# Group norms 1 to 3: mean squares kept in the statistics tile and summed by a second product on TensorE, with the engines' orders written anew

## The reference

```
x = x + block0(gn(x))   # gated line recurrences over rows and columns, with a layer norm
x = x + block1(gn(x))   # maxima of shifted images, 1x1 conv, batch norm, gelu
x = x + block2(gn(x))   # depthwise 11x11 conv with a kernel made of 4 bumps
x = x + block3(gn(x))   # 1x1 conv, 8x8 real FFT filter, 3x3 depthwise, gelu gate, 1x1 conv
def gn(v, G=32, eps=1e-05):
    g = v.reshape(B, G, C // G, H, W)
    m = mean(g, axis=(2, 3, 4)); s = var(g, axis=(2, 3, 4))
    return (g - m) / sqrt(s + eps)
```

## Time and profile before

| | |
|---|---|
| median of 3 runs | 204.95 us (204.21, 204.95, 208.93) |
| the profiled execution | 203.61 us |
| its span in the trace | 201.8 us |
| PE / PEld busy | 172.9 us (86%) / 122.1 us (61%) |
| DVE busy | 171.9 us (85%) |
| ACT / POOL busy | 124.1 us (62%) / 85.8 us (42%) |

### The profile page before, as it was taken

How to read it: one execution, slowest core, us unless ns; L and a number is a source line. 1 busy time by engine, 2 the same in 40 slices (tenths; PEclk the granted TensorE clock), 3 DMA queues, 4 the chain that set the end, 5 groups by cost and what they waited for, 6 DMA issues and landing times. The chain is left out here.

```text
span 201.8 us, 3245 instructions
## 1 busy us (share of the span) xinstructions
PE 172.9 (86%) x852; PEld 122.1 (61%) x852; DVE 171.9 (85%) x436; ACT 124.1 (62%) x272; POOL 85.8 (42%) x173
## 2 busy tenths in 40 slices
PE   2998997988998999999999797499998999986192
PEld 1566564743453884797975486198687788844130
DVE  6678996659987979798999999968999989988792
ACT  3255698669988959779589694053755655361510
POOL 7636237222443244337674777543247490220000
PEclk9999999699799999999999999969999999999559
DMA  5991000000001000000000100011000000101002
GB/s 147 287 229 39 13 16 15 20 20 15 7 8 29 1 10 11 10 20 8 9 7 0 39 0 0 2 44 41 0 3 0 22 17 3 39 2 39 0 0 78
DMA packets 8273, 6.29 MB, mean 31 GB/s; under 512 B 6080, under 2 KB 6848, under 8 KB 8160
## 3 DMA queue, kind: packets, MB, share of 16 engines
q1 hardware_dynamic: 8256, 6.09, 12.0%
HBM read 2.94 MB, written 1.57 MB: 22 GB/s over the span
## 5 line engine op out<-in xcount | busy, mean ns | idle before, releaser
L476 PE MATMUL bank<-xw,bumps 128*128 128x192 f32 x256 | 46.5, 337 | 0.3 <-DVE x L1456 0.3
L476 PEld LDWEIGHTS bank<-xw,bumps 128*128 128x128 f32 x256 | 43.3, 196 | 3.5 <-issue 3.5
L1081 POOL TENSOR_TENSOR msq<-moments 96x2 f32<-96x2 f32 x24 | 7.2, 300 | 45.6 <-DVE moments L1267 45.4
L1128 POOL TENSOR_TENSOR xw<-x_pix,weights 128x384 f32<-128x384 f32 x18 | 17.8, 1014 | 5.6 <-ACT x_pix L840 5.6
L1478 DVE SCALAR_TENSOR_TENSOR bank<-above,weights,bank 112x512 f32<-112x512 f32 x24 | 18.0, 750 | 0.7
L1478 DVE SCALAR_TENSOR_TENSOR bank<-below,weights,bank 112x512 f32<-112x512 f32 x24 | 18.0, 752 | 0.5
L1253 DVE BATCH_NORM_STATS2 stats<-x 96x6 f32<-96x256 f32 x48 | 17.7, 411 | 0.2
L1085 POOL TENSOR_TENSOR rstd<-gvar,weights 96x2 f32<-96x2 f32 x24 | 16.6, 694 | 1.9
L1092 POOL TENSOR_TENSOR ln_rstd<-ln_var,weights 128x4 f32<-128x4 f32 x8 | 8.6, 1078 | 16.6 <-ACT squared L779 16.6
L513 PE MATMUL bank<-prod,weights 128*128 128x512 f32 x16 | 9.9, 703 | 5.4 <-DVE prod L1484 5.3
L389 PEld LDWEIGHTS bank<-weights,v_hs 96*128 96x128 f32 x64 | 10.1, 236 | 5.6 <-issue 4.4
(11 more groups left out here) (174 smaller groups left out, 433.9 us busy)
## 6 DMA issues: line engine op xcount, KB each, us to landing
out_channels<-x_out SPq DMA_DIRECT2D x8, 192.0 KB, 2.1
x_all<-x_channels SPq DMA_DIRECT2D x1, 768.0 KB, 11.4
weights<-weights_packed SPq DMA_DIRECT2D x1, 709.0 KB, 8.4
lines<-strip SPq DMA_DIRECT2D x4, 128.0 KB, 5.4
x_all<-x_channels SPq DMA_DIRECT2D x2, 192.0 KB, 3.7
x_all<-x_channels SPq DMA_DIRECT2D x1, 384.0 KB, 6.6
weights<-weights_packed SPq DMA_DIRECT2D x1, 338.0 KB, 4.7
seq<-gu_col SPq DMA_DIRECT2D x8, 32.0 KB, 2.0
```

The source lines that it names most:

```text
L476: last = mm(p_conv[co][:, 0:NP * C], bumps[:, n, q:q + P8, :].rearrange("p a b -> p (a b)"), xw[j % 2][:, n, ci, :, :].rearrange("p a b -> ...
L1128: tt(xw[j % 2][:, n, :, :, :].rearrange("p a b c -> p (a b) c"), x_pix[j % 2][:, :, :], w("wb")[:, n * C:(n + 1) * C].unsqueeze(1).broadca ...
```

## The change

`norm_squares` is one instruction. It writes 128 times the squared mean into field 0 of `stats`, where BN_STATS had put the count: on DVE as one SCALAR_TENSOR_TENSOR, or on ACT as one Square with a scale. 21 of the 24 are on DVE and 3 on ACT: (1,3), (3,0) and (2,3). The tile `squares` and the second DVE step are not used any more in blocks 1 to 3.

`norm_means` is two products: the means with weights `means`, and the fields 0 and 2 with weights `seconds`, 8 columns each (the moving means are read twice to fill 8). Both weight blocks are new in the packed weights and lengthen the last weight transfer from 1418 to 1610 columns. The first `norm_means` also waits for that transfer. Block 0's norm is as before.

The orders differ in some twenty places. The diff, cut to its core:

```diff
@@ norm_means (PE)
-                pe.wait_ge(s[f"gn{b}_e2"], j + 1)
+                pe.wait_ge(s[f"gn{b}_sq"], j + 1)
...
-                mm(p_gn, w("group", 0, C + 1),
-                   stats[0:C + 1, b - 1, j % 2, :, :].rearrange("p i (f t) -> p (i f) t", f=2)[:, :, 1:3],
-                   start=True, stop=True).then_inc(s[f"gn{b}_group"], 1)
+                if (b, j) == (1, 0):
+                    pe.wait_ge(s["weights_late"], 16)
+                t = stats[0:C + 1, b - 1, j % 2, :, :].rearrange("p i (f t) -> p (i f) t", f=2)
+                mm(p_gn[:, 0:8], w("means", 0, C), t[0:C, :, 1:2].broadcast_to([C, 2 * NP, 2]),
+                   start=True, stop=True)
+                mm(p_gn[:, 8:16], w("seconds", 0, C + 1), t[:, :, 0:3:2], start=True, stop=True
+                   ).then_inc(s[f"gn{b}_group"], 1)
@@ norm_squares (ACT, new)
+            def norm_squares(b, j):
+                act.wait_ge(s[f"gn{b}_stats"], j + 1)
+                after(act, f"gn{b}_sq", j)
+                t = stats[0:C, b - 1, j % 2, :, :].rearrange("p i (f t) -> p (i f) t", f=2)
+                f(t[:, :, 0], t[:, :, 1], ACT.Square, scale=HALF ** 0.5).then_inc(s[f"gn{b}_sq"], 1)
@@ norm_squares (DVE)
-                q = squares[:, b - 1, j % 2, :, :].rearrange("p i f -> p (i f)")
-                tt(q, t[:, :, 1], t[:, :, 1], ALU.mult).then_inc(s[f"gn{b}_sq"], 1)
-                dve.wait_ge(s[f"gn{b}_sq"], j + 1)
-                stt(t[:, :, 2], t[:, :, 2], -2.0 / PIX, q, ALU.mult, ALU.subtract).then_inc(s[f"gn{b}_e2"], 1)
+                stt(t[:, :, 0], t[:, :, 1], HALF * 1.0, t[:, :, 1], ALU.mult, ALU.mult).then_inc(s[f"gn{b}_sq"], 1)
@@ order of PE
             convolve(1, 0)
-            norm_means(1, 3)
             transpose_convolved(0, 0)
             transpose_h1(4)
+            norm_means(1, 3)
...
             output_product3(5)
-            keep_clock_between(1, 8)
             mix_channels3(7)
@@ order of ACT
-            copy_change0(4)
+            norm_squares(1, 3)
+            norm_squares(3, 0)
-            copy_h1(5)
-            copy_convolved(0, 1)
-            copy_states(6)
+            norm_squares(2, 3)
@@ order of DVE
+            copy_change0(4)
-            norm_squares(1, 3)
-            norm_squares(3, 0)
+            copy_h1(5)
+            copy_convolved(0, 1)
+            copy_states(6)
-            norm_squares(2, 3)
+            gate0(6)
             norm_squares(2, 4)
-            gate0(6)
```

More of the change, by code:

```diff
@@ L81, in weight_layout @@
                         ("dbias", 4)]),
-            ("late", [("w1", C), ("w2", 128), ("cb", 1), ("gamma", 1), ("beta", 1), ("mean", 1), ("var", 1),
+            ("late", [("means", C), ("seconds", C), ("w1", C), ("w2", 128), ("cb", 1), ("gamma", 1), ("beta", 1), ("mean", 1), ("var", 1),
                       ("expand", 128), ("filt", C), ("wc", 2 * NPT), ("rad", NPT), ("dx", W), ("bigx", W),
@@ L96, in shape_constants @@
     c["group"] = np.vstack([np.kron(np.eye(32), np.ones((3, 3))) / -6.0, np.full((1, C), -0.5)])
+    same = np.kron(np.eye(32), np.ones((3, 3)))
+    c["means"] = same / -12.0
+    c["seconds"] = np.vstack([same / (3.0 * PIX), np.full((1, C), 0.5)])
     c["root"] = np.full((128, 1), np.sqrt(LN_EPS / C))
@@ L230, in build @@
         GROUP_OF = {0: 1, 1: 2, 2: 3, 4: 4}
-        p_gn = bank[0][0:C, 0:8]
+        p_gn = bank[0][0:C, 0:16]
         p_taps = (bank[6], bank[7])
@@ L604, in _ @@
             convolve(1, 0)
-            norm_means(1, 3)
             transpose_convolved(0, 0)
             transpose_h1(4)
+            norm_means(1, 3)
             transpose_v2(1)
             transpose_convolved(1, 0)
+            gate_product(4)
             project(7)
-            gate_product(4)
             change0(5)
@@ L646, in _ @@
             change0(7)
+            output_product3(0)
             transpose_h1(6)
-            output_product3(0)
             transpose_v2(3)
@@ L662, in _ @@
             transpose_convolved(0, 3)
+            norm_means(2, 5)
             transpose_convolved(1, 3)
-            norm_means(2, 5)
             output_product3(1)
@@ L894, in _ @@
             normalise0(2)
+            gelu_h1(0)
             gates_and_inputs(1)
-            gelu_h1(0)
             place_row_states(0)
             order_rows(1)
+            gelu_h1(1)
             copy_change0(0)
-            gelu_h1(1)
             layer_norm_variance(2)
@@ L917, in _ @@
             normalise0(4)
+            gelu_h1(3)
             tanh_gate0(2)
-            gelu_h1(3)
             normalise0(5)
@@ L1055, in _ @@
             memset(stats0[:, :, :, :].rearrange("p a i (f t) -> p (a i f) t", f=2)[:, :, 2:3], -GN_EPS)
-            memset(stats[:, :, :, :, :].rearrange("p b a i (f t) -> p (b a i f) t", f=2)[:, :, 2:3], -GN_EPS
+            memset(stats[:, :, :, :, :].rearrange("p b a i (f t) -> p (b a i f) t", f=2)[:, :, 2:3], GN_EPS
                    ).then_inc(s["rows_set"], 1)
@@ L1194, in _ @@
             weigh_pixels(2, 4)
+            weigh_pixels(1, 4)
             weigh_pixels(3, 4)
-            weigh_pixels(1, 4)
             norm_factors(2, 5)
@@ L1257, in norm_squares @@
                 dve.wait_ge(s[f"gn{b}_stats"], j + 1)
+                after(dve, f"gn{b}_sq", j)
                 t = stats[0:C, b - 1, j % 2, :, :].rearrange("p i (f t) -> p (i f) t", f=2)
-                q = squares[:, b - 1, j % 2, :, :].rearrange("p i f -> p (i f)")
-                tt(q, t[:, :, 1], t[:, :, 1], ALU.mult).then_inc(s[f"gn{b}_sq"], 1)
-                dve.wait_ge(s[f"gn{b}_sq"], j + 1)
-                stt(t[:, :, 2], t[:, :, 2], -2.0 / PIX, q, ALU.mult, ALU.subtract).then_inc(s[f"gn{b}_e2"], 1)
+                stt(t[:, :, 0], t[:, :, 1], HALF * 1.0, t[:, :, 1], ALU.mult, ALU.mult).then_inc(s[f"gn{b}_sq"], 1)
             def norm_moments(b, j):
@@ L1267, in norm_moments @@
                 nc.vector.tensor_reduce(moments[:, b - 1, j % 2, :, :], p_gn.rearrange(
-                    "p (i f q) -> p q i f", i=NP, f=2), AX.X, ALU.add).then_inc(s[f"gn{b}_moments"], 1)
+                    "p (q i f) -> p q i f", q=2, i=NP), AX.X, ALU.add).then_inc(s[f"gn{b}_moments"], 1)
             def normalise(dst, src, m, r):
@@ L1635, in _ @@
             max_vertical_pairs(0)
+            max_vertical(0)
             max_horizontal(0)
-            max_vertical(0)
             add_block0(1)
@@ L1668, in _ @@
             max_horizontal(2)
+            max_vertical_pairs(2)
             add_block1(1)
-            max_vertical_pairs(2)
             norm_statistics(2, 1)
+            copy_change0(4)
             max_vertical(2)
@@ L1681, in _ @@
             layer_norm_h1(5)
-            norm_squares(1, 3)
             gated_inputs(6)
             add_h1_bias(5)
+            add_block1(2)
             norm_moments(1, 3)
-            add_block1(2)
             norm_statistics(2, 2)
@@ L1834, in _ @@
             tap3(6, 4)
+            tap3(7, 4)
             copy_convolved(1, 6)
-            tap3(7, 4)
             filter_spectrum(5)
```

## The result

The changed kernel takes 208.45 us in the median of its first 4 runs (205.59 to 211.52), the kernel before 204.58 us in its 4 (202.88 to 208.93). Run twelve times more, on another occasion, the changed kernel took 204.88 us against 203.61: 1.0063 (1.0014 to 1.0112). The kernel before, run against itself in the same way, gave 1.0059 (1.0013 to 1.0106). A ratio of 1.006 can therefore not be told from no change. So the times alone say only that the change brings nothing and costs perhaps 1%. I had forecast a gain of 1.2 us, and a median of 199.6 to 207.2 us with 8 chances in 10.

What follows compares the result with a forecast made beforehand. PE was taken to set the pace up to about 88 us, DVE after it. The terms 0.4 + 0.27 - 1.6 + 0.2 - 0.5 = -1.2 us took the median from 204.95 to 203.7; 8 in 10 range 199.6 to 207.2.

Steps and rivals of the forecast that it cites:

- the stall: Squaring of block 2, pair 5, 3.08 us at 125.13, ending with POOL's four weighings; expected again at nearly its length.
- Those between 88 and 131 us fall into PE's free time: PE's added norm products between 88 and 131 us, priced at 0.20 us each elsewhere, were taken to cost nothing there.
- 8 x 0.18 + 0.16 = 1.6 us off DVE where it sets the pace: From 88 to 131 us, eight squarings lose an instruction, one of them going to ACT: 1.6 us gained.
- The 0.27 of `copy_states(6)`: At about 88 us this copy comes to DVE where there is no cover, costing 0.27 us.
- The 0.2 held by POOL: Around 117 us a DVE early at its squaring is held to the end of POOL's weighings, losing some 0.2 us.
- The second term, after 136 us,: Six squarings save DVE 1.1 us; with both engines full, half is kept, a gain of 0.5 us.
- +0.4 for the products: Between 66 and 88 us four added PE products cost 0.8 us, about half covered by waits for ACT, so 0.4.
- nothing for three of the copies: Copies moved to DVE between 66 and 85 us, before waits for PE: costed at nothing, up to 2.1 us if uncovered.
- the waits that I took as cover: Between 66 and 88 us DVE's waits for PE at the norm's reductions, 0.79 and 1.33 us, would hide three copies.
- my signs of being wrong: Far overlong new two-input DVE or POOL instruction; longer DVE wait for L377 or L379, 66-88 us; `mix_channels3(7)` at 1.8 us.
- Rival 3: PE's added products on the path throughout: 17 from 66 to 165 us cost 3.4 us, giving 207.6; chance 0.12.
- Rival 1: One product of zeros gone at 181.10: clock falls before `mix_channels3(7)`, costing 1.4 to 1.5 us, giving 205.2; chance 0.27.
- Rival 2: Stall at 125.13 goes: 2.8 or 2.9 us back, convolution 1.7 more, 5.8 with the 1.2, giving 199.1; chance 0.13.

Runs made afterwards that it cites:

- run 2: Kernel before with the new arithmetic alone (one squaring instruction, second product in norm_means, new matrices), all orders as before: 206.13 us, 1.0122.
- run 4: Changed kernel with the second keep_clock_between(1, 8) put back behind output_product3(5): 205.84 us, without a ratio.
- run 9: Kernel before with norm_means' product issued twice, the first into unused columns of the same bank, nothing else: 205.49 us, 1.0097.
- run 3: Kernel before with the new orders alone (four copies on DVE, one keep_clock_between), old squares and old product: 205.38 us, 1.0068.
- run 11: Kernel before with the new arithmetic, old orders, and squarings (1,3), (3,0), (2,3) and (2,5) on ACT: 199.50 us, 0.9804.
- run 5: Changed kernel with norm_squares(2, 5) moved from DVE to ACT: 201.87 us, 0.990 of the kernel before.
- run 10: Kernel before with the squares of norm (2,5) written by ACT to PSUM, DVE's second instruction kept: 198.44 us, 0.9767.
- run 13: Kernel before with the squares of (2,5) by ACT into PSUM and without the keep_clock_between(1, 8) behind output_product3(5): 198.38 us, 0.9835.
- run 6: Kernel before with the new arithmetic, old orders, and norm_squares(2, 5) on ACT: 200.36 us, 0.9816.
- run 12: Kernel before with the squares of (2,5) and (2,3) by ACT into PSUM, DVE's second instructions kept: 203.22 us, 0.9941.

## Why the prediction was wrong, point by point

The first median, 208.45 us, lies above my range; the repeat's 204.88 lies inside it, but with no gain in either. The stretches show where the sum went wrong.

**What held.** DVE's busy time fell by 1.3 us (forecast 3.4 less some 2), PE's records grew by 46 (48 loads, of which the trace may miss some), the stall came back at nearly its length (3.27 for 3.08), `mix_channels3(7)` takes 1.10 us and the last weights are covered in both traces of the changed kernel: POOL's first step behind them and DVE starts at 14.8 for 14.4 us, and at 14.3 in the second. In runs 2 and 4, with the same weights, POOL did not wait for DVE behind them (that step at 14.6 and 15.3 us), so the cover is thin.

**The step that failed** is the one that reads "Those between 88 and 131 us fall into PE's free time" together with "8 x 0.18 + 0.16 = 1.6 us off DVE where it sets the pace". The products are not free there: 0.34 us (run 9). And DVE gave 0.7 us, not 1.6, by the subtraction under run 9: I took DVE as the pace of the whole stretch because it was busy for 9.87 of 10, but 3 us of that was the held instruction, and a DVE that came early waited for PE or POOL at four places and was held by POOL at three more (run 2). An engine with 3.4 of 10 us free still stands on the path at the handovers.

**The smaller terms there.** The 0.27 of `copy_states(6)` did not show: 45.01 us in run 3 for 44.97 and 44.98. The 0.2 held by POOL came, but in the long stall (3.27 for 3.08 us), not at the weighings from 113 us on, where the changed kernel's squaring took 0.15. And I had no term at all for 131 to 136 us, where the change costs some 0.5.

**The second term, after 136 us,** has the wrong sign. I kept half of DVE's 1.1 us; the runs show +0.75 for the products and nothing for DVE. I had written that five more products are 1.0 us on PE against 0.7 less on DVE; when both engines read as full, the dearer side was the one to count.

**60 to 88 us.** I gave +0.4 for the products and nothing for three of the copies. Run 2 shows -0.3 to +0.2 for the arithmetic there, run 3 puts 0.7 to 1.2 on the orders. These sizes are loose. Over all traces this stretch, (1,2) to (2,2), took 24.05 to 24.90 us in five with the old arithmetic and the old orders up to there, 24.57 to 24.81 in three with the new arithmetic and the old orders (run 11 with two squarings on ACT), and 25.20 to 26.26 in five with the new orders. So the orders cost something here, and the arithmetic's part is not told from nothing. Of the waits that I took as cover that of 0.79 us is gone and that of 1.33 shrank to 0.68, while the one between them, 0.66 before, grew to 0.91 and to 1.09 in the second trace. A longer wait for L379 here was one of my signs of being wrong:

```profile
75.67 0.17 DVE L1276 TENSOR_REDUCE moments<-bank 96x4 f32<-96x16 f32 x1 [0.91 <-PE bank L379]
...
84.17 0.68 DVE L1340 COPY h<-bank 16x512 f32<-16x512 f32 x1 [0.27 <-PE bank L409]
...
86.39 0.17 DVE L1276 TENSOR_REDUCE moments<-bank 96x4 f32<-96x16 f32 x1 [0.68 <-PE bank L379]
```

but PE came later as well, by the 0.3 to 0.8 us of the ruler. That lies inside the 2.1 us that I named as the bound. Which of the moved steps makes PE late was not tried.

**Rival 3** (PE's products on the path throughout, 207.6) is what the runs support in its mechanism: run 9 shows it in every stretch. Its size, 3.4 us, is more than the 2 us measured. I gave it 0.12 because PE was idle for 3.4 us of 120 to 130; 1.8 of that was the stall's (its wait for L1262, 1.80 us at 128.47) and not free time that a product could use.

**Rival 1** (the clock falls earlier at the end). The half of its price that could be seen is right: in run 5 `to_spectrum(7)` took 1.65 us for 0.91, and the end of the span 0.8 us more; `mix_channels3(7)` stayed at 1.10. Its cause is not shown: in the changed kernel the clock fell behind `to_spectrum(7)` as before, and of runs 10 and 13 the one with both products of zeros fell earlier. From the last reduction to the end it took 21.9 to 23.6 us with one and 21.9 to 22.9 with both. One thing speaks for it: `to_spectrum(7)` was longer than 0.92 us in two of the five traces with one product (runs 3 and 5, 1.26 and 1.65) and in none of the nine with both.

**Rival 2** (the stall goes) did not occur by itself, and I had put 5.8 us on it, 1.2 of them for the rest of the change and so 4.6 for the stall and its clock. Made to occur (run 10), it gives 3.06 us up to (2,5) and 1.7 or 2.1 behind it, 4.8 to 5.1 in all. That price was nearly right.

**The port.** I had weighed the Trainium skill (SBUF — State Buffer, Who interferes with whom), by which the one that issues first keeps the port for its whole instruction, against a DVE instruction held for all of four. The runs go with the trace: 3.08 us in the three kernels with the old squaring (before, runs 3 and 9) and 3.27 in the three with the new one (after, runs 2 and 4), to the end of the fourth weighing. The same section's statement that a DVE instruction with at most one SBUF input does not contend, outside the 2-port modes, agrees: 0.15 us in run 10 with one of the two in PSUM.

## What to carry to other kernels

Before costing a change at an engine that reads as full, take out of its busy time the instructions that are only held; here one of 0.15 us read as 3.08 and also cost PE its clock, and moving it alone was worth 4.8 us, four times the gain that I had forecast for the whole change. A saving on one of two engines that hand work to and fro is worth what the other one's waits leave of it, and work added to the other is on the path at the handovers even where that engine shows idle time. If half of a step is handed to another engine, ask first what stands behind the half that stays: it waits in order.

## What the runs showed of the hardware that I had not expected

- Two distances between the same steps repeat to 0.04 us from trace to trace, while the times of one kernel spread over 201.3 to 210.2 us. Much of the spread arises in the first 60 us, and the granted clock has a part in it: in run 6 it was low from 37.5 to 54.5 us and (1,2) came at 66.4 us, in all other traces at 58.9 to 62.8. It is not the whole cause: with no low stretch (1,2) came at 58.9 us in run 2 and at 61.1 in run 12, and with 10 us of low clock before 30 us at 59.5 in run 10. Two traces tell effects of 0.2 us that six to twelve timed runs of each kernel do not.
- A 96x4 instruction on DVE with two inputs from SBUF is held for a whole run of four instructions on POOL (3.08 to 3.27 us), though each of those ends by itself after 1.0 us (0.98 to 1.32).
- The low clock after PE had idled 1.8 to 2.2 us lasted 3.4 or 6.8 us for the same kernel, and cost 1.7 or 2.1 us of the (2,5) to (3,3) distance (5.65 or 6.04 for 3.98 at the full clock). In run 3, where it came earlier, 3.4 us of it cost that distance only 0.5 (4.47).
